# Eight scatters of a chunk sent in one step of a window instead of two in each of four steps, in a two-layer graph network kernel

## What is computed

```
src, dst = ...                                   # 212,500 edges
h = relu(layernorm(x))
x = x + layer0(h, edges into dst, edge_attr_4, edge_attr_16)
h = relu(layernorm(x))
w = relu(edge_attr_64 @ W_fc1) @ W_fc2           # 224 weights per edge, second layer
sh = sqrt(3) * edge_attr_3 / norm(edge_attr_3)
x = x + layer1(...)   # products of w, h[dst] and sh, summed by src, then node matrices, silu and gates
```

## Time and profile before

| what | value |
|---|---|
| median of 3 runs | 9630.93 us (9630.51 to 9639.42) |
| the profiled execution, its own time | 9623.72 us |
| its span, first to last instruction | 9622.0 us |
| mean granted TensorE clock over the span | 0.822 |
| PE, DVE, ACT, POOL busy over the span | 72%, 75%, 51%, 72% |
| instructions | 170,670 |
| DMA over the span | 137 GB/s |

### The profile page before, as it was taken

The page is one execution under the profiler, slowest core; times in us unless marked ns, Lnnn a source line. Parts: engine busy times, 40 slices in busy tenths (PEclk is TensorE's granted clock), DMA queues, the critical chain, the costliest instruction groups (busy, mean ns, idle before and its releaser), DMA issues. The chain is left out here.

```text
span 9622.0 us, 170670 instructions
## 1 busy us (share of the span) xinstructions
PE 6909.3 (72%) x31166; PEld 4531.3 (47%) x31166; DVE 7250.6 (75%) x21188; ACT 4950.1 (51%) x16490; POOL 6942.6 (72%) x7069
## 2 busy tenths in 40 slices
PE   5666666655666666666666666668789999999999
PEld 3333333332222222222222222245578888888889
DVE  7565665665777777777777777777789999999995
ACT  3444444443444444444444444434467777777774
POOL 4777777777777777777777777756677777777770
PEclk8655555567888888888888888888899999999999
DMA  2222222224444444444444444445456666666667
GB/s 90 92 92 92 92 91 92 92 90 124 138 138 136 137 138 137 137 136 135 138 137 137 137 138 138 130 138 158 153 159 168 169 168 167 168 171 167 170 166 210
DMA packets 826473, 1315.62 MB, mean 137 GB/s; under 512 B 228520, under 2 KB 627624, under 8 KB 826280
## 3 DMA queue, kind: packets, MB, share of 16 engines
q0 software_dynamic: 337920, 667.48, 24.7%
q1 hardware_dynamic: 417496, 547.30, 18.8%
q10 hardware_dynamic: 70992, 100.14, 3.0%
HBM read 862.45 MB, written 914.08 MB: 185 GB/s over the span
## 5 line engine op out<-in xcount | busy, mean ns | idle before, releaser
L1445 POOL DMA_INDIRECT feat_m<-feat_tab,rows_m x3712 | 3653.1, 984 | 1155.3 <-issue 997.9
L1578 ACT ACTIVATE prod_m<-part_m,rows_m 128x64 f32<-128x64 f32 x5568 | 1432.4, 337 | 2197.5 <-DVE part_m L1768 2141.2
L1545 PE MATMUL pair<-prod_m,hot_m 128*128 128x160 f32 x14848 | 2243.5, 304 | 159.2 <-DVE prod_m L1751 119.7
L1545 PEld LDWEIGHTS pair<-prod_m,hot_m 128*128 128x128 f32 x14848 | 2043.4, 190 | 359.4 <-issue 358.2
L1522 PE MATMUL bank<-prod_m,hot_m 128*128 128x449 f32 x2476 | 1424.3, 709 | 944.6 <-DVE prod_m L1788 795.7
L1566 ACT ACTIVATE hot_m<-hot_m,rows_m 128x128 f32<-128x128 f32 x5568 | 1728.7, 389 | 693.1 <-DVE hot_m L1734 687.9
L652 POOL DMA_INDIRECT sorted_rows<-rows_e,place_e x1664 | 1614.4, 970 | 532.1 <-issue 505.2
L1464 POOL DMA_INDIRECT sorted_rows<-later_m,place_m x1248 | 1262.4, 1012 | 380.4 <-issue 345.3
L1522 PEld LDWEIGHTS bank<-prod_m,hot_m 128*128 128x128 f32 x2476 | 542.7, 241 | 1840.1 <-issue 1629.0
L1751 DVE TENSOR_TENSOR prod_m<-rows_m,feat_m 128x192 f32<-128x192 f32 (+2 forms) x4640 | 1316.4, 323 | 0.0
L1768 DVE TENSOR_TENSOR part_m<-rows_m,feat_m 128x128 f32<-128x128 f32 x928 | 271.1, 292 | 1015.1 <-DMA feat_m<-feat_tab,rows_m 1012.1
(11 more groups left out here) (250 smaller groups left out, 10209.4 us busy)
## 6 DMA issues: line engine op xcount, KB each, us to landing
agg_tab<-acc_m ACTq DMA_DIRECT2D x928, 320.0 KB
rows_m<-sorted_rows SPq DMA_DIRECT2D x928, 229.0 KB
agg_tab<-acc_m ACTq DMA_DIRECT2D x928, 224.5 KB
rows_m<-sorted_rows SPq DMA_DIRECT2D x928, 197.0 KB
feat_m<-feat_tab,rows_m POOLq DMA_INDIRECT x3712
turned_m<-in_turned ACTq DMA_DIRECT2D x159, 256.0 KB
agg_s<-agg_tab SPq DMA_DIRECT2D x98, 320.0 KB, 3.3
sorted_rows<-rows_e,place_e POOLq DMA_INDIRECT x1664, 2.4
```

The lines of the kernel that those rows point to most:

```text
L1445: pool.indirect_dma_start(out=feat[s % RING][:, k, :], out_offset=None, in_=g.feat_tab[l.n], in_offset=bass.IndirectOffsetOnAxis(ap=rows[s ...
L1545: mm = pe.matmul(dst, hot[s % l.hot_bufs][:, k, q, :], rhs, start=(k == 0 and col == 0), stop=(k == ST_TILES - 1), skip_group_check=True)
L1578: ins = act.activation(prod[s % prods][:, k, at:at + S0], part[s % 2][:, k, 0:S0], ACT.Copy, scale=rows[s % HELD][:, k, l.sh_at + m:l.sh_a ...
```

## The change

All eight scatters of a chunk are sent in part 2 of the window, behind the same waits; parts 3, 4 and 5 send nothing. The order in a window is then, from part 2: `SSSSSSSS GG GG GG GG GG GG`.

```diff
                 if s not in WINDOW:
                     return
-                j, i = WINDOW[s][0], WINDOW[s][1] - 2
-                if i < 0:
+                j, part_ = WINDOW[s]
+                if part_ != 2:
                     return
                 h, c = (j - 1) % 2, it * PER_TURN + j - 1
-                if i == 0:
-                    pool.wait_ge(copied, c + 1)
-                    pool.wait_ge(evicted, c * 4 + 4)
-                    pool.wait_ge(r.place_here, c + 1)
-                    settle(pool, g.passed)
-                for k in (2 * i, 2 * i + 1):
+                pool.wait_ge(copied, c + 1)
+                pool.wait_ge(evicted, c * 4 + 4)
+                pool.wait_ge(r.place_here, c + 1)
+                settle(pool, g.passed)
+                for k in range(CHUNK_TILES):
                     pool.indirect_dma_start(
                         out=g.sorted_rows[1], out_offset=bass.IndirectOffsetOnAxis(ap=place[h][:, k:k + 1], axis=0),
                         in_=later[h][:, k, :], in_offset=None).then_inc(sent[h], 16)
```

## The result

The median of six runs is 9578.1 us (9572.3 to 9588.5), against 9632.2 us of six runs of the kernel before: the medians are 54 us apart. The ratio of the runs is 0.9946 with a 95% interval of 0.9933 to 0.9959, which of 9632 us makes 52 us. Timed again beside later experiments it gave 9579.5 us and 0.9951 (0.9938 to 0.9963). The forecast was 9583 us. The profiled execution has a span of 9570.5 us, 51.5 less than before.

The account below looks back on a forecast made before the run. GpSimd's issuing was taken to bound the first-message stage. Saving 0.31 us in each of 155 windows makes 48 us: 9630.9 − 48 = 9583 us, likeliest 9555 to 9610, with the range reaching up to 9632 us.

Parts of the forecast that it names:

- the slack of the slots: Ahead of each burst, ScalarE's slots would be written 6.8 us early instead of 14.5, so no wait arises.
- the waits at the stage's end: GpSimd's waits in the first-message stage would still have 0.3 us as the longest; none was named at its end.
- GpSimd sets the stage's length: The first-message stage lasts as long as GpSimd's list of instructions, 25.9 us a window, since GpSimd never stops.
- The size: 0.31 us a window, 48 us: GpSimd's gathers and scatters in a window would take 25.21 us instead of 25.52, over 155 windows.
- Waits for ScalarE over 0.3 us at the scatters' line: A sign, in front of GpSimd's scatters, that the prediction would be wrong.
- The price of changing kind: On GpSimd, pairs after the other kind take longer (gathers 2.55 against 2.50 us); three of four changes each way go.
- All of the excess: Rival and upper bound: GpSimd's mean excess tied to changes goes, 0.64 us a window, 99 us, 9532 us; chance 0.05.
- nothing: Rival and lower bound: the hundredths on GpSimd have another origin and the burst keeps them, 9631 us; chance 0.10.
- The cover of the burst: VectorE's longer wait for gathered rows behind eight scatters stays hidden: about 6.4 us idle a window, in one piece.
- Rows late behind the burst: Rival: scatters run one by one in the DMA queue, GpSimd stands 2.2 us a window, +293 us, 9924 us; chance 0.05.
- TensorE's clock: Rival: after longer waits TensorE stays at the low clock, 26.3 us a window, stage 62 us longer, 9693 us; chance 0.04.

Follow-up runs that it names:

- part 5 of the own window: The changed kernel with the burst three steps earlier, in part 5 of the chunk's own window: 10077.8 us, ratio 1.0457 to the kernel before.
- alternating: The kernel before with scatter and gather alternating one by one in parts 2 to 5: 9600.0 us, ratio 0.9989.
- grouping by four: The changed kernel with four scatters in part 2 and four in part 4: 9587.7 us, ratio 0.9977 to the kernel before.
- grouping by sixteen: The changed kernel with both chunks of a turn sent together in part 2 of the next turn: 9578.0 us, ratio 0.9964 to the kernel before.
- part-0 kernels: The changed kernel with the burst in part 0 of the next window, plain (9710.4 us, 1.0087) or with one more edit (1.0103, 1.0101, 1.0083 to the kernel before).

## Why the prediction was right

The time, the direction and the mechanism came as forecast: GpSimd's instructions became shorter by what stands before them, and all of it but 6.4 us reached the stage's end. Two of its smaller readings, the slack of the slots and the waits at the stage's end, did not come true.

- *GpSimd sets the stage's length.* Right. It stood for nothing but 0.3 us of issuing before and after, and each kernel's measured time follows its own issuing time in the table above. Where it had to wait, in part 5 of the own window, the whole wait came out at the end.
- *The size: 0.31 us a window, 48 us.* The body gave 0.33 us, 52 us, and the two waits at the end of the stage, which the prediction did not name, took 6.4 us of it back. It said that the last chunk has no gathers between, but not that the burst of the chunk before it then has no gathers to hide its slots behind. Waits for ScalarE over 0.3 us at the scatters' line were its own sign of being wrong; they came, twice in 1248 scatters, and cost too little to matter. That the size came out so near is in part luck: the kind alone is worth 46 us, the instructions beside VectorE's work gave some 6 more, which the prediction left as they were, and the end took 6.4 back. The stage is 45.4 us shorter in the one recording and 48.5 in the other.
- *The price of changing kind.* Right for the three changes that the change takes away, wrong as the rule that I made of it. The prediction compared each row with its predecessor, which was enough; the first expectation went on to a price per change, and alternating (expected +64 us, measured −11) showed that the ceiling had been reached. The rule failed by its form: the price hangs on the two instructions ahead, and is smaller for each where kinds alternate. The forecast did not use the rule, as it took each row's own time.
- *The bounds.* "All of the excess" (99 us) and "nothing" (0) both missed; the rows that compare neighbours were the right ones to take, as the instructions beside an idle VectorE show with the same hundredths.
- *The cover of the burst.* VectorE idles in one piece (4.7 us behind the burst shown, 6.3 at most) where 6.4 was said; its waits for gathered rows are fewer and longer, 147 over 4 us instead of 71, and their total is a little less, 932 us against 991 over the like stretch. The slots, in ScalarE's timeline:

```profile
3044.97 0.21 ACT L1625 ACTIVATE place_m<-rank_f_m 128x8 int32<-128x8 f32 x1
```

  They are written at 3045.18 and the burst begins at 3053.13, 8.0 us later; over the windows of the body it is 6.9 to 8.8 us, median 8.6, where 6.8 was said. The gathered rows came sooner behind the burst than the 3.6 us taken: in the burst shown 2.3 us after the second gather was issued (3040.01 to 3042.33).
- *Rows late behind the burst* did not happen: the wait in front of the first products was 6.3 us at the longest, and GpSimd showed no wait for it.
- *TensorE's clock.* The rival was that it would stay at 1.2 GHz. It did not stay there: one group of matmuls runs low and the next high, see below.

## What to carry to other kernels

When one engine issues without a pause and the rest wait for it, ask what each instruction costs behind its neighbour: some 0.017 us in the mean, twenty times a window in 155 windows, was the whole effect here. Rows of one kind are cheaper than pairs, but fully so only from the third on, so grouping by four gave about half and grouping by sixteen no more than eight, with other engines then waiting for the buffers. And a burst can't be moved freely even where its waits are satisfied: in one place the same eight scatters cost 130 us more. Read the mean duration of the bottleneck's own instructions, and not its waits alone.

## What was not expected

**TensorE's matmuls ran less often at the low clock.** It now waits longer in one piece, 6.65 us in the row below, and yet its busy time in the stage went from 2592 us to 2390. The stage's mean granted clock is no measure of it: 0.83 before, 0.84 here and 0.83 in the second recording of the changed kernel, and 0.86 with alternating kinds, where TensorE was busy longer than here. TensorE's timeline after such a wait:

```profile
3044.48 3.33 PE L1521 MATMUL bank<-prod_m,hot_m 128*128 128x449 f32 x4 [6.65 <-DVE prod_m L1787]
...
3049.25 1.67 PE L1521 MATMUL bank<-prod_m,hot_m 128*128 128x449 f32 x4
```

One group of four matmuls at the low rate (3.33 us, 1.2 GHz), the next at the high one (1.67 us, 2.4 GHz). Before, the low rate held over two groups in the window shown; this is the second of them, behind only 0.62 us of idle time:

```profile
3012.93 3.33 PE L1522 MATMUL bank<-prod_m,hot_m 128*128 128x449 f32 x4 [0.62 <-DVE prod_m L1788]
```

From 2300 to 6200 us, 239 of 899 such groups of four took over 3 us before, 156 of 911 after, and 165 of 911 in the second recording. The waits have been put together: TensorE's idle pieces over 0.3 us went from 683 to 529, while their sum grew from 1380 to 1558 us. It gained nothing at the end, as TensorE doesn't set the stage's length. The Trainium skill (TensorE: Matmul & The Clock Gate, HAM oscillation) warns of bursts of matmuls between waits for DMA; here the larger bursts are the better case, which agrees with its advice to keep the matmuls together.

**The same scatter takes 0.96 or 1.5 us.** In each of the part-0 kernels 93 to 108 scatters took at least half a microsecond more, the idle time in front of them being the usual 0.3 us for nearly all; the 200 in the expectation above is too many. The Trainium skill (GPSIMD Engine Reference, its specifications) says that GpSimd shares its SBUF interfaces with VectorE, with contention for instructions of two SBUF inputs. The products that overlap the long scatters are of that sort. They overlap short ones as well (201 of the changed kernel's scatters overlap all three, none of them longer than 1.25 us), so no run here shows that this is the cause.
